# Softmax reciprocals turned by VectorE and spread through DRAM by two DMAs, in a fused cross-attention and feed-forward kernel

## The reference

```python
q = norm(x) @ wq + bq;  k = ctx @ wk + bk;  v = ctx @ wv + bv      # 16 heads of 32
score = (q @ k.T) / sqrt(32) * mask
score = where(score == 0, -1e9, score)
x = x + (softmax(score) @ v) @ wo + bo
x = x + real(ifft(fft(norm(x)) @ w)) + bias                        # w complex 512 x 512
```

## Time and profile before

| | |
|---|---|
| time before, median of 3 runs | 458.94 us (458.43 to 459.73) |
| the profiled execution | 458.93 us |
| its span in the trace | 457.1 us |
| busy share of TensorE, VectorE, ScalarE, GpSimd | 97%, 87%, 82%, 79% |

### The profile page before, as it was taken

How to read it: one execution, slowest core, us unless ns; L and a number is a source line. 1 busy time by engine, 2 the same in 40 slices (tenths; PEclk the granted TensorE clock), 3 DMA queues, 4 the chain that set the end, 5 groups by cost and what they waited for, 6 DMA issues and landing times.

```text
span 457.1 us, 11172 instructions
## 1 busy us (share of the span) xinstructions
PE 442.1 (97%) x3510; PEld 293.3 (64%) x3510; DVE 398.0 (87%) x630; ACT 372.6 (82%) x1434; POOL 359.6 (79%) x540
## 2 busy tenths in 40 slices
PE   6989898999999999999999999999999999999997
PEld 5777686777666666666666666666666666555444
DVE  3797699899999999999999999999999898999443
ACT  3358597789999999898989898989989888899720
POOL 6588744795889899998989898869899685976663
PEclk9999998999999999999999999999999999999999
DMA  8996752332445454545555445445433334330344
GB/s 288 392 368 182 236 195 71 97 86 71 90 92 142 122 147 115 152 110 143 128 134 138 116 107 148 91 114 147 115 96 70 97 74 98 70 93 13 82 104 126
DMA packets 85287, 60.16 MB, mean 132 GB/s; under 512 B 40141, under 2 KB 72813, under 8 KB 84718
## 3 DMA queue, kind: packets, MB, share of 16 engines
q1 hardware_dynamic: 84508, 59.29, 47.3%
q10 hardware_dynamic: 722, 0.17, 0.2%
HBM read 29.33 MB, written 8.39 MB: 83 GB/s over the span
## 4 chain that ended last, share of the span: by engine, by line
PE 79%; DVE 10%; issue 5%; ACT 3%; DMA 1%; ACTq 0%; POOL 0%; DVEq 0%
PE bank L438 32%; PE bank L525 17%; PE bank L582 10%; PE bank L599 6%; PE scores L570 5%; PE bank L443 4%; DVE zs L867 3%; PE bank L595 3%; DVE zs L860 1%; ACT zs L688 1%; DMA bqb<-in_bq 1%; PE scores L443 1%; DVE cn L883 1%; ACT pt L697 1%; DVE x L845 1%
## 5 line engine op out<-in xcount | busy, mean ns | idle before, releaser
L688 ACT ACTIVATE zs<-zs,nbias 128x128 f32<-128x128 f32 x512 | 199.6, 397 | 8.2 <-POOL nbias L1093 7.9
L688 ACT ACTIVATION_READ_ACCUMULATOR zs<-zs,nbias 128x1 f32 x512 | 99.4, 194 | 0.0
L867 DVE SCALAR_TENSOR_TENSOR zs<-zs 128x1024 f32<-128x1024 f32 x64 | 81.3, 1270 | 0.2
L872 DVE TENSOR_REDUCE nmin<-zs 128x8 f32<-128x1024 f32 x64 | 78.1, 1220 | 2.2
L860 DVE TENSOR_TENSOR zs<-scores,ms 128x1024 f32<-128x1024 f32 x64 | 78.0, 1218 | 0.3 <-issue 0.3
L525 PE MATMUL bank<-xth,wqh 128*128 128x256 f16 x256 | 70.9, 277 | 4.0 <-DVE kl L810 2.0
L697 ACT COPY pt<-bank 128x512 f32<-128x512 f32 x128 | 68.4, 586 | 6.7 <-PE bank L582 6.3
L525 PE MATMUL bank<-xtl,wqh 128*128 128x256 f16 x256 | 70.4, 275 | 0.0
L525 PE MATMUL bank<-xth,wql 128*128 128x256 f16 x256 | 70.4, 275 | 0.0
L582 PE MATMUL bank<-ident,zs 128*128 128x128 f32 x512 | 67.5, 275 | 0.7 <-ACT zs L688 0.7
L1053 POOL TENSOR_TENSOR xs<-xs,bob 128x512 f32<-128x512 f32 (+1 forms) x41 | 42.4, 1036 | 24.5 <-DVE zs L867 24.5
(11 more groups left out here) (118 smaller groups left out, 960.1 us busy)
## 6 DMA issues: line engine op xcount, KB each, us to landing
xs<-in_x SPq DMA_DIRECT2D x16, 512.0 KB, 4.2
xtr<-in_xt SPq DMA_DIRECT2D x16, 512.0 KB, 4.4
out<-x SPq DMA_DIRECT2D x31, 256.0 KB, 2.6
qs<-qh SPq DMA_DIRECT2D x120, 64.0 KB
lp<-in_lparts SPq DMA_DIRECT2D x4, 1024.0 KB, 9.0
qs<-ql SPq DMA_DIRECT2D x60, 64.0 KB
ms<-in_mask SPq DMA_DIRECT2D x16, 128.0 KB, 2.6
wqs<-in_wq SPq DMA_DIRECT2D x2, 512.0 KB, 6.8
```

The source lines that it names most:

```text
L688: last = act.activation(z, z, ACT.Exp, bias=nbias[:, s % 4, i:i + 1], scale=-NEG, accum_out=zsum[:, s % 4, i:i + 1])
L867: dve.scalar_tensor_tensor(out=z, in0=z, scalar=0.0, in1=z, op0=ALU.is_equal, op1=ALU.subtract).then_inc(eq_done, 1)
L872: dve.tensor_reduce(nmin[:, s % 4, :], zs[:, s % NZ].rearrange("p t h k -> p (t h) k"), AX.X, ALU.min).then_inc(mn_done, 1)
```

## The change

The two transposes by TensorE, the copy by GpSimd and the copy by ScalarE go. Instead:

- VectorE takes the reciprocals between `zero_to_neg` and `least`, into 8 of 32 columns, and behind `least` it transposes the 32 x 32 blocks of that 128 x 32 tile (`turn_rz`).
- One DMA (`lay_rows`) writes the turned tile to a DRAM buffer, so that each of its rows holds one head's reciprocals of 128 tokens. A second DMA (`spread_rows`) reads 8 of those rows and writes `rec`, each head's 256 values to that head's 32 partitions.
- For items 0 to 3 (`SA = 4`) ScalarE issues both, `lay_rows` at the end of step `s + 2` and `spread_rows` at the start of step `s + 3`; from item 4 on SP does, `spread_rows` and then `lay_rows` at the start of its steps. `spread_rows` waits until `lay_rows` has landed, and `ctx_norm` until `spread_rows` has.
- `stack_q` is no longer issued in one piece: 3 of its DMAs stand in step r = 3, 3 behind everything of r = 0, and 6 with the two of `stack_rows` in r = 1.

```diff
+        def lay_rows(eng, s):
+            eng.wait_ge(rz_done, s + 1)
+            if s >= 4:
+                eng.wait_ge(d_rr[s % 2], 16 * ((s - 4) // 2 + 1))
+            eng.dma_start(rows[s % 4].rearrange("i (p q) -> p i q", p=4),
+                          rzt[:, s % 2, :]).then_inc(d_rw[s % 2], 16)
+        def spread_rows(eng, s):
+            eng.wait_ge(d_rw[s % 2], 16 * (s // 2 + 1))
+            if s >= 2:
+                eng.wait_ge(cn_done, s - 1)
+            eng.dma_start(rec[:, s % 2], rows[s % 4, 0:8].rearrange("(j t) p -> j (t p)", t=2).unsqueeze(1).broadcast_to([4, 32, CH])
+                          ).then_inc(d_rr[s % 2], 16)
...
             for v in range(V0, V1):
                 c, r = divmod(v, 4)
+                if SA <= v - 3 < NS:
+                    spread_rows(sp, v - 3)
+                if SA <= v - 2 < NS:
+                    lay_rows(sp, v - 2)
...
-                    stack_q(c + 2)
+                    stack_q(c + 2, [0])
+                if r == 0 and 3 <= c + 1 < NC:
+                    stack_q(c + 1, [1])
+                if r == 1 and 3 <= c + 1 < NC:
+                    stack_q(c + 1, [2, 3])
...
-                pe.wait_ge(p_rz, s + 1)
-                for t in range(2):
-                    pe.transpose(CX[:, 256 + 128 * t:384 + 128 * t],
-                                 rzb[:, s % 2, 4 * t:4 * t + 4, :], ident[:])
...
-                if 0 <= v - 4 < NS:
-                    copy_rec(v - 4)
+                if 0 <= v - 3 < SA:
+                    spread_rows(act, v - 3)
...
+                if 0 <= v - 2 < SA:
+                    lay_rows(act, v - 2)
...
+            def turn_rz(s):
+                dve.wait_ge(r8_done, s + 1)
+                if s >= 2:
+                    dve.wait_ge(d_rw[s % 2], 16 * (s // 2))
+                dve.transpose(rzt[:, s % 2, :], rz[:, s % 2, :]).then_inc(rz_done, 1)
             def ctx_norm(s):
-                dve.wait_ge(rc_done, s + 1)
+                dve.wait_ge(pv_done, s + 1)
+                dve.wait_ge(d_rr[s % 2], 16 * (s // 2 + 1))
...
+                if 0 <= v - 2 < NS:
+                    recip(v - 2)
                 if 0 <= v < NS:
                     least(v)
+                if 0 <= v - 2 < NS:
+                    turn_rz(v - 2)
...
-                if 0 <= v - 2 < NS:
-                    recip(v - 2)
```

More of the change, by code:

```diff
@@ L21 @@
 VS = 9
-VP = 4
+SA = 4
 LAST = ("FF", NC - 1, 1)
@@ L196, in build @@
         zsum, _ = sb("zsum", [128, 4, 8], F32)
-        rz, _ = sb("rz", [128, 4, 8], F32)
+        rz, _ = sb("rz", [128, 2, 32], F32)
+        rzt, _ = sb("rzt", [128, 2, 32], F32)
         us, a_us = sb("us", [128, 4, D], F32)
@@ L227, in build @@
         d_o = [sem(f"d_o{i}") for i in range(NO)]
+        d_rw = [sem(f"d_rw{i}") for i in range(2)]
+        d_rr = [sem(f"d_rr{i}") for i in range(2)]
         d_eye, d_cx, d_wv, d_wo, d_bb = (sem(f"d_{n}") for n in ("eye", "cx", "wv", "wo", "bb"))
@@ L249, in build @@
         p_l1, p_l2, p_zero = (sem(n) for n in ("p_l1", "p_l2", "p_zero"))
-        p_const, p_ms, p_nb, p_cl, p_st, p_xb, p_r2, p_x1b, p_sm, l_done, p_rz = (
-            sem(n) for n in ("p_const", "p_ms", "p_nb", "p_cl", "p_st", "p_xb", "p_r2", "p_x1b", "p_sm", "l_done", "p_rz"))
+        p_const, p_ms, p_nb, p_cl, p_st, p_xb, p_r2, p_x1b, p_sm, l_done = (
+            sem(n) for n in ("p_const", "p_ms", "p_nb", "p_cl", "p_st", "p_xb", "p_r2", "p_x1b", "p_sm", "l_done"))
         hi_count = {}
@@ L311, in row @@
             return v.rearrange("(o n) -> o n", o=1).broadcast_to([128, D])
+        rows = nc.dram_tensor("rz_rows", (4, 32, 128), F32, kind="Internal").ap()
+        def lay_rows(eng, s):
[10 more added lines that the diff above has]
+                          ).then_inc(d_rr[s % 2], 16)
         block = stack.enter_context(nc.Block())
@@ L332, in load_mask, with stack_q @@
                 sp.dma_start(ms[:, c % NM], m_d[:, c]).then_inc(d_m[c % NM], 16)
[L334 to L338, removed]
+            def stack_q(c, heads=range(4)):
+                if 0 in heads:
+                    sp.wait_ge(g_free, at["Q", c, 3] + 1)
+                    if c >= 2:
+                        sp.wait_ge(sc_done, 2 * (4 * (c - 2) + 3) + 2)
+                for j in heads:
                     stack_head(sp, c, j)
-                if c >= 2:
+                if c >= 2 and 3 in heads:
                     stack_rows(sp, c)
@@ L697, in copy_pt @@
                 act.copy(pt[:, s % 2, 2 * f:2 * f + 2, :], PB[f][:]).then_inc(pt_copied, 1)
-            def copy_rec(s):
-                act.wait_ge(pv_done, s + 1)
-                act.copy(rec[:, s % 2, :], CX[:, 256:512]).then_inc(rc_done, 1)
             def ctx_hi(s):
@@ L876, in recip @@
                 dve.wait_ge(ex_done, s + 1)
-                dve.reciprocal(rz[:, s % 4, :], zsum[:, s % 4, :]).then_inc(rz_done, 1)
+                dve.reciprocal(rz[:, s % 2, 0:8].rearrange("p (j t) -> p t j", t=2),
+                               zsum[:, s % 4, :].rearrange("p (t j) -> p t j", t=2)).then_inc(r8_done, 1)
+            def turn_rz(s):
[3 more added lines that the diff above has]
+                dve.transpose(rzt[:, s % 2, :], rz[:, s % 2, :]).then_inc(rz_done, 1)
             def ctx_norm(s):
-                dve.wait_ge(rc_done, s + 1)
+                dve.wait_ge(pv_done, s + 1)
+                dve.wait_ge(d_rr[s % 2], 16 * (s // 2 + 1))
                 if s >= 2:
@@ L953, in _ @@
             dve.memset(bqb[:], 0.0).then_inc(b_zero, 1)
+            dve.memset(rz[:], 1.0).then_inc(b_zero, 1)
             low_q(0)
@@ L1176, in _ @@
                     constant_row()
-                if v <= VP and 0 <= v - 3 < NS:
-                    spread(v - 3)
                 for a in range(5, NC):
@@ L1224, in _ @@
                         split_lo(a)
-                if v >= VP and 0 <= v - 2 < NS:
-                    spread(v - 2)
                 if r == 0 and 2 <= c + 1 < NC:
```

8 lines of the change are left out of this document (1 added, 7 removed).

## The result

The changed kernel takes 536.21 us (median of 4 runs, 533.28 to 540.57), the kernel before 459.29 us beside it (458.43 to 459.73). The ratio is 1.169, with a 95% interval from 1.162 to 1.176. The direction was as predicted (487 us, range to 508), but the cost is 77 us, not 28.

What follows compares the result with a forecast made beforehand. TensorE bounds the kernel before; SP's queue with two latencies was to bound the changed one, 27.35 us a chunk. 458.9 + 29.1 (chunks) - 3.7 (other steps) + 3 (start) = 487 us, range 456 to 508.

Steps and rivals of the forecast that it cites:

- TensorE's transposes: On TensorE's path, two transposes of the reciprocals go: 0.23 us a step, 14.7 us over 64 steps if nothing takes over.
- VectorE's part: VectorE's moved reciprocal (0.18 us) and new transpose (0.2 us, ends 0.1 and 0.4) were taken to cost zero.
- SP's queue: SP from `lay_rows` of r = 3 to next chunk's `spread_rows` of r = 2: 18.1 us old DMAs, 3.25 new issues.
- The loop's way back: From `spread_rows` of r = 2 through `ctx_norm` to `lay_rows` of r = 3: 3.0 landing, 3.0 VectorE; loop 27.35 us.
- The landing of `rec`: The 128 KB of `spread_rows` were taken to land in 3.0 us, ends 1.7 and 4.2.
- third rival: Second DMA slow on few engines: loop 1.2 us longer, 28.55, and the time 502 us; chance 0.22.
- The chunk of before: Four steps of the kernel before, bound by TensorE, were taken at 24.62 us, so a chunk grows by 2.7 us.
- The start: In steps 3 to 6 ScalarE issues both DMAs and waits out the landing between: 3 us lost, ends 0 and 6.
- The other steps' gain: The 16 steps outside the twelve looped chunks keep TensorE as bound: 16 x 0.23 = 3.7 us less.
- The first: Rival: the DMAs are hidden, TensorE stays the bound, and the kernel is faster, 447 us; chance 0.15.
- The second: Rival: no change, the loop from its low ends, 24.45 us, to 25.0, giving 456 to 463 us; chance 0.08.
- The fourth: Rival: TensorE slows down after its new waits; at 1 us a chunk the time is 499 us; chance 0.05.

Runs made afterwards that it cites:

- e6: Changed kernel without the two new DMAs, `ctx_norm` multiplying by a constant tile (sums left out), `stack_q` whole: 447.2 us, ratio 0.974 to the kernel before.
- e13: Changed kernel with both small DMAs issued by ScalarE (second in mid-step), `stack_q` whole, 16 source rows for the second DMA: 449.9 us, ratio 0.982.
- e1: Changed kernel with four buffers for the constant rows (`srow`) instead of two, nothing else: 513.8 us, ratio 1.120 to the kernel before.
- e3: Changed kernel with reciprocals repeated in all 32 columns, so the second DMA's source has 16 slowest rows instead of 4: 534.9 us, ratio 1.166.
- e4: Changed kernel with four `srow` buffers and 16 instead of 4 source rows for the second DMA: 501.9 us, ratio 1.094 to the kernel before.
- e12: Changed kernel with only both small DMAs moved to ScalarE (second in mid-step) and `stack_q` whole; two row buffers, four source rows: 456.8 us, ratio 0.997.
- e10: Changed kernel with both small DMAs on ScalarE (second in mid-step), `stack_q` whole, four `srow` buffers, 16 source rows: 449.9 us, ratio 0.982.
- e7: e1 with `ctx_norm` multiplying by a constant tile, so nobody else waits for `rec`; SP still issues both DMAs: 487.7 us, ratio 1.063.
- e15: e10 with the second DMA at the start of ScalarE's step instead of its middle: 522.3 us, ratio 1.140 to the kernel before.
- e8: e4 with SP issuing the second DMA in mid-step, a step earlier, and `ms`, a store and `xtr` moved from r = 0 to r = 2: 474.9 us.
- e2: Changed kernel with `stack_q` issued in one piece in step r = 3 again: 585.0 us, ratio 1.275 to the kernel before.
- e14: e12 with four `srow` buffers, still four source rows for the second DMA: 456.9 us, ratio 0.996 to the kernel before.

## Why the prediction was right or wrong, point by point

- **TensorE's transposes**, 0.23 us each, 14.7 us if nothing takes over: e6 gives 11.4. From item 8 to item 56 it gains 10.8 us, close to 48 x 0.23 = 11.0; the other 16 steps, where I had taken 3.7, give less than 1.
- **VectorE's part.** The reciprocal and the transpose take 0.20 us each (0.18 and 0.2 taken), and what follows starts 0.13 us behind each. Right, and at no cost in e13, where TensorE is the bound.
- **SP's queue.** The count was right: 18.1 + 3.25 = 21.35 us from `lay_rows` of r = 3 to `spread_rows` of r = 2, and 1.1 less in the last three chunks, a mean of 21.1; by SP's timeline the mean of the twelve is 21.3, from 19.7 to 23.2. In the chunk shown above it is 295.02 - 272.01 = 23.0. The new issues take 0.54 to 0.60 us and a gap of some 0.05, as taken; the 1.65 more of this chunk is one transpose of 2.41 instead of 1.26, one `xtr` of 1.05 instead of 0.43 us and 0.35 in which SP stands still at 279.00, less the 0.5 that I had allowed.
- **The loop's way back**: here the prediction failed. It said "then `ctx_norm` on VectorE may run", 3.0 us of landing and 3.0 us of VectorE, and so that "This is a closed loop" of 27.35 us. The same DMAs of SP have a second way back, which I didn't follow: the split of `stack_q`, which I costed only by its place in SP's list, moves the constant row's DMAs to one step ahead of ScalarE's copy into the same buffer. From the end of SP's list, at 295.02, that way takes 9.1 us until the next `lay_rows`, instead of 3.0 + 3.0. It makes this chunk 32.1 us where the prediction had 27.35; 1.65 of these 4.8 are SP's, and 3.1 the way back. Over the twelve chunks the way back has a mean of 8.8 us (9.1 to 9.3 in nine of them, in the last three 8.3, 7.7 and 6.9), where the prediction had 6.0: 34 us in all. In e1 the mean is 7.1, so some 20 of these are ScalarE's row and some 13 the predicted way itself, longer than I took it (this is counted from `lay_rows` to `lay_rows`; the sum below goes by `ctx_norm`, which shifts it a little). e1 removes the row's way (-22 us), e3 and e4 confirm it. VectorE's timeline of the changed kernel says the same: in ten of the twelve chunks it doesn't wait in front of the `ctx_norm` of r = 3, where the prediction closed its loop and named the missing wait as the sign that this step fails.
- **The landing of `rec`**: 3.0 taken, 3.8 to 4.7 in the middle of e1's chain, and e1's way back is 1.1 us over the 6.0, so the third rival's 1.2 us more was nearer; e4 puts the few source rows at 12 us of time where the loop runs through `rec` (the rival: 14.4). What the runs show is, behind the constant rows, 3.8 to 4.0 us in e1 with 4 rows in the slowest dimension and 2.8 to 3.0 in e4 with 16; 6.02 us in e12's chain with 4, and in e13 with 16 a median of 2.7, with 5.2 at most. The Trainium skill, DMA: Bandwidth & Descriptors, section "Why a DMA increments its semaphore by 16 and not by 1", ties the number of engines to that dimension. The times agree in direction; no view here gives the number of engines itself, and the place of the DMA among the others makes as large a difference.
- **The chunk of before.** I took 24.62 us from one chunk. That holds for the six in the middle; the mean over twelve is 24.1, and SP's own chunk was 181.11 - 157.11 = 24.0 already. This alone is 12 x 0.5 = 6 us of missing cost.
- **The start**: 3 us taken (ends 0 and 6), 4.9 measured. In steps 3 to 6 ScalarE waited 2.17, 5.90, 2.21 and 1.66 us for the landings, where I had taken 2.0 each. In e13 item 8 is back at 116.14 us (before: 115.92): the mid-step place costs the start next to nothing.
- **The other steps' gain** of 3.7 us isn't there: 78.1 us of span less 70.6 and 4.9 leaves 2.6 lost. e6 shows that there was less than 1 us to gain, since TensorE isn't the bound in these steps; and VectorE's timeline puts 2.4 of the 2.6 between items 60 and 63, where it waits 1.90 us for `rec` in front of item 61.

The terms add up like this, for the profiled span. Predicted: 29.1 + 3 - 3.7 = 28.4. Measured, 78.1: for the chunks 41.5 more (6 the chunk of before, 23 ScalarE's row, by e1's mean chunk of 28.07 against 30.0, and 12 the rest of e1's over the predicted 27.1), for the start 1.9, for the other steps 6.3.

**The rivals.** The first, 447 us with hidden DMAs, didn't come in this kernel, and SP was where it failed; 449.9 us was reached once SP was out of it. The second's low ends were nowhere near. The fourth was half seen: the granted clock fell to 0.97 and 0.93 of its upper level (2.4 GHz) in the two stretches above, from 1.00, and TensorE was busy 450.2 us, where e10 has 428.7 for the same 3382 instructions at 1.00 in its stretch. The chain has TensorE at 10% only, so most of these 21.5 us are time in which it would have waited; no run isolates it.

**The signs.** VectorE's wait before `ctx_norm` was there, 48.9 us, but in steps r = 1 and 2, not in 1 and 3. TensorE's share was 81% in the middle, not 87%. SP had its pauses in front of `lay_rows` of r = 3 (304.12) and of the `spread_rows` ahead of it (299.17), where it waits for the `lay_rows` of r = 2 to land, as named.

## What to carry to other kernels

When a change moves instructions on a queue, list for each moved one who waits for it, the engine that wants to overwrite its source too, and how many buffers that source has. A buffer's release by a DMA is a wait like any other, and a loop that was found is not yet the longest one: with a bound removed (e1, e7), the next stood only some 2 us a chunk behind (22 and 26 us over twelve chunks). Small DMAs with someone waiting belong on a queue that comes to them in time, at a place where their own wait has already ended; where in ScalarE's step the second one stood was worth 72 us (e10 against e15). What the queue is worth by itself no pair of runs shows. Queue, place and `stack_q` together gave 79 us (e12 against the changed kernel); with the second DMA in mid-step on either queue it was 25 (e8 against e10, in which `stack_q` and the step of the second DMA differ too).

## What the runs showed of the hardware

- A DMA that ScalarE issues behind its exponentials takes 0.55 us, while exponentials that stand ahead of it go on without a gap (e10, 260.39). With nothing left to run ahead of it, the next exponential starts 0.60 us behind the start of the issue (e10, 256.61).
- The landing of the same 128 KB varied from 2.3 us (e13, 16 rows in the source's slowest dimension) to 6.15 (e2) and 6.91 (e14), both with 4 rows; with 16 rows the longest was 6.1 (e10). At one place in SP's list 16 rows took about 1 us less than 4 (e4 against e1). The long ones of e2 and e12 stand close behind loads of 512 KB, in e12 on another queue. A size alone doesn't give it.
- The second DMA isn't the only latency: `rz_rows<-rzt`, 16 KB, took 4.85 us in e12 and 4.34 in e8.
- GpSimd took 762 ns to issue a DMA that SP and ScalarE issued in 0.55 us.
